# TensorE turns the identity while it waits: 40 transposes ahead of the projection and 42 at the passage to attention

## The chip, the cores and the metric

The kernel runs on one core of a Trainium2 chip. The metric is the device time of one execution in microseconds (us), the median of several runs. In what follows PE is TensorE, PEld its weight loads, ACT ScalarE, DVE VectorE, POOL GpSimd and SP SyncE, which issues most of the DMAs.

## What is computed

A transformer layer over x of 2 x 2048 rows of 256 floats, all in float32: attention with 16 heads of 16, then a mixing projection and a mixture of 8 experts of which each row takes 2, with a layer norm behind each half.

```python
qkv = x @ qkv_w + qkv_b                      # 256 -> 16 heads x (16 q, 16 k, 16 v)
q, k = rot(q), rot(k)                        # the angle depends on the head alone
attn = softmax(q @ k.T / 4)                  # per head, 2048 x 2048
x = layernorm(x + (attn @ v) @ out_w + out_b)
n = layer_norm(x, g1, be1); x2 = x + n + n @ mix_w + mix_b
flat = layer_norm(x2, g2, be2)
combine = top-2 weights of softmax(flat @ router_w)
y = sum over e of combine[:, e] * (silu(flat @ w1[e] + b1[e]) @ w2[e] + b2[e])
out = layernorm(x + x2 + y)
```

## The kernel before

The program has three blocks, one behind the other. At the end of a block every engine drains its work and raises a semaphore; POOL collects these and releases all five engines together. Whoever drains last sets when the next block begins.

**project** (line 176). SP loads rows of x and `qkv_w`; DVE turns the rows (`turn_x`), copies the weights of v and rotates those of q and k in 16 passes (`rotate`: the two 128-row chunks first, then the bias row). PE waits at first for `wv_ready` (the copy of v's weights), multiplies v for the first 512 rows (`take_v(0)`, line 487), then waits for the first `weights_rotated`, takes q of the first rows (`take_qk`, line 497), waits for the second `weights_rotated`, and turns the bias by four transposes (line 538). After that eight groups of 512 rows go through PE, ACT, DVE and POOL, which split q and k in three bf16 parts that SP stores to HBM. POOL makes the identity in its first two microseconds. At the end PE turns `b_in` (line 557) and multiplies a flag (line 559); DVE makes of it `wide`; SP waits until the stores of the parts have landed (lines 239 and 240).

**maxima** (line 600). SP, PE and DVE each load `wide` into a register and branch over the block's body if it is zero, as with this data. ACT and POOL have nothing to do in it.

**attend_route_experts**. PE scores two heads by 512 queries at a time: 8 matmuls of 32 keys each (line 1521) into one of three PSUM buffers; ACT takes the exponential of 128 x 1024 (line 1429) into a ring of six slots; PE weighs v by them (line 1533), 4 matmuls for each exponential, and between these come jobs for the rest of the layer (line 1549). There are 1024 such steps. SP loads the heads of k and q from HBM in the first steps (lines 732, 741, 1063). Behind attention come 71 tiles of the experts (lines 1663, 1676, with transposes at 1542 and 1647), and the last layer norm.

PE's order at the head of attention is written out by hand: four increments of semaphores (lines 1697 to 1700), three scores ahead, and then `attend`, which for each step waits for the exponential, scores three steps ahead and weighs.

Of the kernel before, what the change touches and what calls it, by code (L numbers as in the profile page):

```python
# [15 lines left out]
P = 128  # L16
# [57 lines left out]
def project(nc, dram, keep, hi_all):  # L74

    with ExitStack() as stack:
# [42 lines left out]
        p_qk = [m.ps(f"p_qk{i}", [P, 512]) for i in range(4)]  # L120
# [8 lines left out]
        identity_ready = m.sem("pj_identity_ready")  # L129
# [34 lines left out]
        x_rows = dram["x"].rearrange("b s c -> (b s) c")  # L164
        identity, v_all = keep["identity"], keep["v_all"]
        V_EARLY = QC

        def tokens(g):

# [6 lines left out]
        with nc.Block() as block:  # L176
# [162 lines left out]
            def _(dve):  # L339
# [105 lines left out]
                for g in range(GROUPS):  # L445
# [10 lines left out]
                    if g + 2 < GROUPS:  # L456
                        turn_x(g + 2)
                    if g + 1 < V_EARLY:
                        for i in range(2):
                            add_v(g + 1, i)  # L460
                add_v(V_EARLY, 0)
                read_norms(GROUPS - 1)
# [13 lines left out]
            @block.tensor  # L476
            def _(pe):
                def take_v(g, halves=range(2)):

                    pe.wait_ge(xT_ready, g + 1)  # L480
                    for i in halves:
                        if g:
                            pe.wait_ge(v_ready, 2 * (g - 1) + i + 1)
                        for a in range(2):
                            tok = (2 * i + a) * P
                            for kc in range(KC):
                                last = nc.tensor.matmul(p_v[i][:, a, :], xT[g][:, kc, tok:tok + P],
                                                        w_v[:, kc, :], start=(kc == 0), stop=(kc == KC - 1))
                        last.then_inc(v_done, 1)

                def take_qk(g, ft):

                    if g:
                        pe.wait_ge(rest_ready, 4 * (g - 1) + ft + 1)
                    pe.wait_ge(xT_ready, g + 1)
                    for kc in range(KC):
                        last = nc.tensor.matmul(p_qk[ft][:, :], w_qk[:, kc, ft, :], xT[g][:, kc, :],  # L497
                                                start=(kc == 0), stop=(kc == KC - 1))
                    last.then_inc(qk_done, 1)

                def take_norms(g):

                    if g:
                        pe.wait_ge(norms_read, 2 * g)
                    pe.wait_ge(q_squared, 2 * g + 2)
                    pe.wait_ge(k_squared, 2 * g + 2)
                    for out, first in ((p_x[0], 2), (p_x[1], 0)):
                        for kc in range(KC):
                            last = nc.tensor.matmul(out[:, :], select[:, kc, :, :].rearrange("p r h -> p (r h)"),
                                                    squares[:, g % 2, first + kc, :],  # L510
                                                    start=(kc == 0), stop=(kc == KC - 1))
                    last.then_inc(normed, 1)

                def average(b):

                    pe.wait_ge(mean_ready, b + 1)
                    if b == 0:
                        pe.wait_ge(v_ready, 2 * V_EARLY - 1)
                    else:
                        pe.wait_ge(rest_ready, 4 * GROUPS)  # L520
                    for kc in range(KC):
                        for c in range(QC):
                            last = nc.tensor.matmul(p_mean[b][32 * c:32 * c + 32, :], key_mean[:, b, kc, :],
                                                    hi_all[:, kc, tokens(b * QC + c)],
                                                    start=(kc == 0), stop=(kc == KC - 1))
                    last.then_inc(averaged, 1)

                pe.wait_ge(wv_ready, 1)
                take_v(0)
                pe.wait_ge(weights_rotated, 1)  # L530
                for g in range(GROUPS):
                    take_qk(g, 0)
                    take_qk(g, 1)
                    if g == 0:
                        pe.wait_ge(weights_rotated, 2)
                        pe.wait_ge(identity_ready, 2)
                        for ft in range(4):
                            last = nc.tensor.transpose(p_qk[3][:, ft * P:(ft + 1) * P], w_qk[:, KC, ft, :], identity[:, :])
                        last.then_inc(bias_turned, 1)
                        pe.wait_ge(filled, 7)  # L540
                        pe.wait_ge(bias_ready, 1)
                    if g:
                        take_norms(g - 1)
                    take_qk(g, 2)
                    take_qk(g, 3)
                    if g == QC + 1:
                        average(0)
                    if g + 1 < V_EARLY:
                        take_v(g + 1)
                pe.wait_ge(mean_read, 1)  # L550
                take_v(V_EARLY, (0,))
                take_norms(GROUPS - 1)
                take_v(V_EARLY, (1,))
                average(1)
                take_v(V_EARLY + 1)
                pe.wait_ge(loaded_b1, 16)
                nc.tensor.transpose(p_qk[2][:, 0:P], b_in[:, :], identity[:, :]).then_inc(b1_turned, 1)
                pe.wait_ge(narrow_ready, 1)
                nc.tensor.matmul(p_qk[1][:, 0:1], ones[:, :], narrow[:, :], start=True, stop=True).then_inc(counted, 1)

def quad(q):
# [13 lines left out]
def maxima(nc, dram, keep):  # L576

    with ExitStack() as stack:
# [9 lines left out]
        p_s = [m.ps(f"mx_s{i}", [P, S]) for i in range(2)]  # L589
# [10 lines left out]
        with nc.Block() as block:  # L600

            @block.sync
            def _(sp):
                wide = sp.value_load(keep["wide"][0:1, 0:1], min_val=0, max_val=P)
                with sp.If(wide > 0):
                    sp.wait_ge(keep["stored_mid"][1], 16 * QC)
                    sp.sem_inc(stored, 16)
                    sp.sem_inc(parts_turned, 1)
                    with sp.Fori(0, BH) as bh:
                        sp.wait_ge(parts_turned, bh + 1)  # L610
                        load_head(sp, dram, bh, q_rows, k_rows, loaded)
                        sp.wait_ge(row_ready, bh + 1)
                        sp.dma_start(dram["negmax"][bass.ds(bh, 1), :, :].rearrange("o t (a n) -> (o t a) n", n=P),
                                     turned[:, :]).then_inc(stored, 16)
                    sp.wait_ge(stored, 16 * (BH + 1))
                    sp.dma_start(keep["q_rows"][0][ROWS:ROWS_M, :, :],
                                 dram["negmax"][0:QUAD, :, 0:512].rearrange("h t n -> t h n")).then_inc(stored, 16)
                    sp.wait_ge(stored, 16 * (BH + 2))

            @block.tensor  # L620
            def _(pe):
                wide = pe.value_load(keep["wide"][0:1, 0:1], min_val=0, max_val=P)
                with pe.If(wide > 0):
                    with pe.Fori(0, BH) as bh:
                        pe.wait_ge(loaded, (bh + 1) * (16 * 12))
                        for qt in range(KT):
                            if qt >= 2:
                                pe.wait_ge(reduced, bh * KT + qt - 1)
                            for c in range(QC):
                                last = nc.tensor.matmul(p_s[qt % 2][:, c * 512:(c + 1) * 512],  # L630
                                                        q_rows[0:ROWS, qt * P:(qt + 1) * P],
                                                        k_rows[0:ROWS, c * 512:(c + 1) * 512], start=True, stop=True)
                            last.then_inc(scored, 1)
                        pe.wait_ge(parts_ready, bh + 1)
                        nc.tensor.transpose(p_turn, columns[:, :],
                                            keep["identity16"][:, :]).then_inc(parts_turned, 1)
                        pe.wait_ge(row_ready, bh + 1)
# [110 lines left out]
def attend_route_experts(nc, dram, keep):  # L748
# [24 lines left out]
    with ExitStack() as stack:  # L773
# [11 lines left out]
        p_s = [m.ps(f"at_s{i}", [P, PAIR * 512]) for i in range(BUFFERS)]  # L785
        p_o = m.ps("at_po", [P, 512])
        small = m.ps("at_small", [P, 512])
# [139 lines left out]
        identity = keep["identity"]  # L927
# [65 lines left out]
        with nc.Block() as block:  # L993
# [517 lines left out]
            def _(pe):  # L1511
# [186 lines left out]
                pe.sem_inc(o_copied, 1)  # L1698
                pe.sem_inc(small_read, 1)
                pe.sem_inc(h_ready, 4)  # L1700
                for n in range(BUFFERS):
                    score(0, n)
                attend(0, False, False, 0)
# [421 lines left out]
```

## Time and profile before

| | |
|---|---|
| median of 3 runs | 1629.89 us (1628.8 to 1631.36) |
| the profiled execution's own time | 1633.76 us |
| its span, first to last instruction | 1632.1 us |
| PE busy, share of the span | 96% |
| ACT busy | 75% |
| DVE busy | 36% |
| POOL busy | 28% |
| mean granted clock of TensorE | 0.987 |

### The profile page before, as it was taken

The page shows a single profiled execution, that of the slowest core. Times are in us where ns is not written, and L with a number is a line of the kernel's source. Part 1 is how long each engine was busy: PE and PEld are TensorE (multiplying, and loading weights), DVE is VectorE, ACT ScalarE, POOL GpSimd, SP SyncE. Part 2 cuts the span into 40 slices and gives each one's busy share as a digit, 9 for nine tenths or more (in the row PEclk, how much of TensorE's full clock was granted, in tenths as well). Part 3 has the DMA queues.
Part 4 walks back from the last instruction along what each step waited for, and adds up shares of the span by engine and source line. Part 5 has one row for each costly group of instructions (what it writes and reads, how often), then busy time and mean ns, then how long its engine had stood idle before and what let it go on. Part 6 is the DMA issues. An engine that isn't in the chain of part 4 may idle for free.

```text
span 1632.1 us, 46348 instructions
## 1 busy us (share of the span) xinstructions
PE 1565.6 (96%) x17759; PEld 920.5 (56%) x17763; DVE 594.6 (36%) x1515; ACT 1227.1 (75%) x1818; POOL 463.2 (28%) x431
## 2 busy tenths in 40 slices
PE   7989999999999999999999999999999999999990
PEld 4443433344334334334434434378899999999990
DVE  6641221553553554544544446443630000000004
ACT  4669999999999999999999999953343343433332
POOL 4730010121321221221221221133546444444441
PEclk9999999999999999999999999999999999999995
DMA  6896210220212552321221211869779876667645
GB/s 172 223 166 85 52 41 12 67 57 20 85 57 66 115 111 60 121 57 38 67 57 38 69 55 38 238 173 199 179 169 236 199 201 179 185 191 194 186 111 212
DMA packets 187563, 195.13 MB, mean 120 GB/s; under 512 B 97161, under 2 KB 159433, under 8 KB 187209
## 3 DMA queue, kind: packets, MB, share of 16 engines
q1 hardware_dynamic: 173587, 174.39, 39.3%
q0 software_dynamic: 13296, 17.77, 6.7%
q8 instruction: 128, 2.10, 0.6%
q10 hardware_dynamic: 495, 0.41, 0.1%
q14 instruction: 57, 0.47, 0.1%
HBM read 141.16 MB, written 47.00 MB: 115 GB/s over the span
## 4 chain that ended last, share of the span: by engine, by line
PE 87%; DVE 2%; issue 2%; ACT 2%; DMA 1%; POOL 0%; DVEq 0%; POOLq 0%; ACTq 0%
PE at_s L1521 26%; PE at_po L1533 26%; PE at_s L1663 16%; PE at_s L1676 15%; PE at_small L1549 4%; ACT place L1429 2%; DVE cb_ln_stats L688 1%; DVE late L714 1%; DMA rows_out<-place,at_v 0%; DVE at_o L1752 0%; PE at_po L1647 0%; DMA place<-rows_out 0%; DVE place L1969 0%; PE at_small L1542 0%; ACT place L1446 0%
## 5 line engine op out<-in xcount | busy, mean ns | idle before, releaser
L1429 ACT ACTIVATE place<-at_s 128x1024 f32<-128x1024 f32 x1024 | 950.4, 1119 | 16.8 <-PE at_s L1521 9.5
L1521 PE MATMUL at_s<-place 99*32 99x512 bf16 x8192 | 570.3, 381 | 7.3 <-PEq L600 5.1
L1533 PE MATMUL at_po<-place,at_v 128*32 128x512 f32 x4096 | 534.9, 594 | 6.3 <-DVE at_o L1752 4.3
L1521 PEld LDWEIGHTS at_s<-place 99*32 99x32 bf16 x8192 | 222.6, 96 | 437.0 <-issue 249.0
L1446 ACT ACTIVATE place<-at_s,b_turned 128x128 f32<-128x128 f32 x568 | 162.0, 369 | 146.1 <-PE at_s L1663 139.4
L1663 PEld LDWEIGHTS at_s<-ex_xT,place 128*128 128x128 f32 x2272 | 264.1, 192 | 7.6 <-issue 3.6
L1663 PE MATMUL at_s<-ex_xT,place 128*128 128x128 f32 x2272 | 265.7, 275 | 1.5 <-issue 1.5
L1676 PE MATMUL at_s<-place 128*128 x1136 | 257.3, 380 | 1.4 <-issue 0.7
L1676 PEld LDWEIGHTS at_s<-place 128*128 128x128 f32 x1136 | 210.4, 190 | 28.1 <-issue 2.4
L1533 PEld LDWEIGHTS at_po<-place,at_v 128*32 128x32 f32 x4096 | 131.7, 111 | 105.5 <-POOL at_v L1267 7.6
L1462 ACT ACTIVATE place<-at_s,at_v 128x256 f32<-128x256 f32 x71 | 33.7, 474 | 160.7 <-PE at_s L1676 148.3
L1950 DVE STREAM_TRANSPOSE ex_xT<-at_v 128x256 f32<-128x256 f32 x53 | 23.5, 445 | 333.1 <-PE at_s L1663 313.4
L1267 POOL COPY at_v<-place 128x1024 f32<-128x1024 f32 x32 | 33.4, 1046 | 385.4 <-PE at_po L1533 330.4
L1389 POOL DMA_INDIRECT rows_out<-place,at_v x71 | 113.4, 1597 | 66.1 <-POOL place L1384 53.9
L1384 POOL TENSOR_TENSOR place<-place 128x256 f32<-128x256 f32 x71 | 52.7, 742 | 207.6 <-ACT place L1462 207.3
L1762 DVE RECIPROCAL at_den<-at_den 128x512 f32<-128x512 f32 x32 | 107.3, 3353 | 1.1
L1305 POOL DMA_INDIRECT rows_in<-rt_sent_rows,rt_pos x64 | 64.3, 1005 | 126.0 <-PE at_po L1533 120.5
L1775 DVE TENSOR_TENSOR late<-at_small,rt_total 128x512 f32<-128x512 f32 x32 | 22.1, 692 | 211.5 <-PE at_small L1549 205.2
L1379 POOL TENSOR_TENSOR place<-place,at_v 128x256 f32<-128x256 f32 x71 | 80.2, 1129 | 17.6 <-issue 16.5
L1752 DVE COPY at_o<-at_po 128x512 f32<-128x512 f32 x32 | 22.1, 692 | 145.3 <-PE at_po L1533 142.7
L1289 POOL TENSOR_TENSOR rt_total<-late 128x1024 f32<-128x1024 f32 x7 | 16.7, 2391 | 159.6 <-DVEq L1887 159.6
L295 ACT ACTIVATE place<-p_qk,bias_qk 128x512 bf16<-128x512 f32 x32 | 21.8, 684 | 34.5 <-PE p_qk L497 22.8
(219 smaller groups left out, 949.3 us busy)
## 6 DMA issues: line engine op xcount, KB each, us to landing
place<-in_w SPq DMA_DIRECT2D x61, 1024.0 KB, 11.6
place<-in_w SPq DMA_DIRECT2D x72, 256.0 KB
place<-k_parts SPq DMA_DIRECT2D x48, 256.0 KB, 4.6
place<-q_parts SPq DMA_DIRECT2D x186, 64.0 KB
at_v<-rows_in SPq DMA_DIRECT2D x212, 32.0 KB
late<-kept SPq DMA_DIRECT2D x52, 128.0 KB, 2.6
place<-in_x SPq DMA_DIRECT2D x32, 128.0 KB, 3.2
at_heads_T<-at_o SPq DMA_DIRECT2D x128, 32.0 KB
```

The lines of the kernel that those rows point to most:

```text
L1305: nc.gpsimd.indirect_dma_start(out=dram["rows_in"], in_=sent_rows[:, n, a, :], in_offset=None, out_offset=bass.IndirectOffsetOnAxis(ap=pos ...
L1379: nc.gpsimd.tensor_tensor(biased[:, :], b2[:, bass.ds(e, 1), :].rearrange("p o n -> p (o n)"), rows_now[:, r, D + 1:D + 2].broadcast_to([P ...
L1384: nc.gpsimd.tensor_tensor(y[:, u, :], y[:, u, :], biased[:, :], ALU.add).then_inc(y_ready, 1)
L1389: nc.gpsimd.indirect_dma_start(out=dram["rows_out"], in_=y[:, u, :], in_offset=None, out_offset=bass.IndirectOffsetOnAxis(ap=rows_now[:, r ...
L1429: nc.scalar.activation(probs[:, slot(i, n), :], scores(i, n)[:, :], ACT.Exp).then_inc(exp_done, 1)
L1446: last = nc.scalar.activation(hT[:, u, fc, :], p_h[u][:, fc, :], ACT.Silu, bias=keep["b1"][:, bass.ds(e, 1), fc])
L1521: last = nc.tensor.matmul(scores(i, n)[j:j + 32, s * 512:(s + 1) * 512], k_rows[0:ROWS_M, quad(q).start + h, kt * P + j:kt * P + j + 32], ...
L1533: last = nc.tensor.matmul(p_o[32 * h:32 * h + 32, :], v_one[q % 2][:, h, kt, :], probs[:, slot(i, q * NG + g), s * 512:(s + 1) * 512], sta ...
L1549: last = nc.tensor.matmul(out[j:j + 32, :], weights[:, j:j + 32], moving, start=start, stop=stop, skip_group_check=lone)
L1663: last = nc.tensor.matmul(p_h[u][:, fc, :], w1_now[slot][:, kc, fc * P:(fc + 1) * P], xT[:, u, kc, :], start=(kc == 0), stop=(kc == KC - 1))
L1676: last = nc.tensor.matmul(p_y[u][:, :], hT[:, u, fc, :], w2[:, bass.ds(e, 1), fc, :].rearrange("p o n -> p (o n)"), start=(fc == 0), stop= ...
L1762: v.reciprocal(den[:, :], den[:, :]).then_inc(den_ready, 1)
```

## The change

Four places get transposes of the identity by itself whose results nobody reads: 40 in `project` as soon as POOL has made the identity, ahead of the wait for `wv_ready`; 18 at the end of `project`, behind the last matmul; 8 ahead of the load of `wide` in `maxima` and 8 behind it, ahead of the branch; 8 in the last block between the increments and the first score.

```diff
+        WARMING = 40
...
+                pe.wait_ge(identity_ready, 2)
+                for _ in range(WARMING):
+                    nc.tensor.transpose(p_qk[3][:, 0:P], identity[:, :], identity[:, :])
                 pe.wait_ge(wv_ready, 1)
                 take_v(0)
...
                 nc.tensor.matmul(p_qk[1][:, 0:1], ones[:, :], narrow[:, :], start=True, stop=True).then_inc(counted, 1)
+                for _ in range(18):
+                    nc.tensor.transpose(p_qk[3][:, 0:P], identity[:, :], identity[:, :])
...
             @block.tensor
             def _(pe):
+                for _ in range(8):
+                    nc.tensor.transpose(p_s[1][:, 0:P], keep["identity"][:, :], keep["identity"][:, :])
                 wide = pe.value_load(keep["wide"][0:1, 0:1], min_val=0, max_val=P)
+                for _ in range(8):
+                    nc.tensor.transpose(p_s[1][:, 0:P], keep["identity"][:, :], keep["identity"][:, :])
                 with pe.If(wide > 0):
...
                 pe.sem_inc(h_ready, 4)
+                for _ in range(8):
+                    nc.tensor.transpose(small[:, 0:P], identity[:, :], identity[:, :])
                 for n in range(BUFFERS):
                     score(0, n)
                 attend(0, False, False, 0)
```

## Rows read from the trace of the kernel before

**Rows 1.** The page: busy time by engine, and a group of instructions.

```profile
PE 1565.6 (96%) x17759; PEld 920.5 (56%) x17763; DVE 594.6 (36%) x1515; ACT 1227.1 (75%) x1818; POOL 463.2 (28%) x431
...
L1429 ACT ACTIVATE place<-at_s 128x1024 f32<-128x1024 f32 x1024 | 950.4, 1119 | 16.8 <-PE at_s L1521 9.5
```

**Rows 2.** Windows on PE: length, PE busy (count), clock, DMA share, GB/s.

```profile
10.81:14.74 3.93, 3.93 (x9) 1.00 1.01 268
14.74:16.45 1.71, 1.71 (x9) 1.00 0.22 48
```

**Rows 3.** Timeline, 0 to 21 us: start, length, engine, line, operation, count, idle before.

```profile
1.43 0.53 POOL L249 TENSOR_SCALAR_AFFINE_SELECT identity<-identity 128x128 f32<-128x128 f32 x2 [0.24 <-POOL identity L246]
...
15.22 0.42 DVE L376 TENSOR_TENSOR w_qk<-rot_a,rot_b 128x256 f32<-128x256 f32 x1
...
16.29 3.60 PE L497 MATMUL p_qk<-place,w_qk 128*128 128x512 f32 x8
...
19.77 0.29 DVE L376 TENSOR_TENSOR w_qk<-rot_a,rot_b 128x128 f32<-128x128 f32 x1
...
20.12 0.66 PE L538 MATMUL p_qk<-identity,w_qk 128*128 128x128 f32 x4 [0.24 <-DVE w_qk L376]
```

**Rows 4.** The end of project, line 176: duration in ns, start in us.

```profile
L176 PEldq DRAIN  x1: 1272/1272/1272, 98.5 to 98.5; - x1
...
L176 SPq DRAIN  x1: 7/7/7, 102.0 to 102.0; - x1
```

**Rows 5.** The same for maxima, lines 622 and 600.

```profile
L622 PEldq TENSOR_LOAD <-wide x1: 496/496/496, 102.3 to 102.3; - x1
...
L600 PEldq DRAIN  x1: 64/64/64, 103.6 to 103.6; - x1
L600 DVEq DRAIN  x1: 70/70/70, 103.8 to 103.8; - x1
```

**Rows 6.** Timeline of PE in the experts' stage.

```profile
1089.30 1.28 PE L1663 MATMUL at_s<-ex_xT,place 128*128 128x128 f32 x10
1090.42 0.60 PE L1542 MATMUL at_small<-identity,rt_sent_rows 128*128 128x128 f32 x4
```

**Rows 7.** Line 1671, a register load of PE there, in the same microseconds.

```profile
L1671 PEldq TENSOR_LOAD <-tile_expert x1: 308/308/308, 1089.1 to 1089.1; - x1
```

**Rows 8.** Timeline of PE and ACT at the head of attention.

```profile
104.85 5.31 PE L1521 MATMUL at_s<-place 99*32 99x512 bf16 x48 [5.10 <-PEq L600]
...
105.94 6.73 ACT L1429 ACTIVATE place<-at_s 128x1024 f32<-128x1024 f32 x7 [0.38 <-PE at_s L1521]
112.93 11.22 ACT L1429 ACTIVATE place<-at_s 128x1024 f32<-128x1024 f32 x12 [0.27 <-PE at_s L1521]
124.33 9.27 ACT L1429 ACTIVATE place<-at_s 128x1024 f32<-128x1024 f32 x10 [0.18 <-PE at_s L1521]
136.82 1.94 ACT L1429 ACTIVATE place<-at_s 128x1024 f32<-128x1024 f32 x2 [3.22 <-PE at_s L1521]
139.02 1.94 ACT L1429 ACTIVATE place<-at_s 128x1024 f32<-128x1024 f32 x2 [0.26 <-PE at_s L1521]
141.18 123.79 ACT L1429 ACTIVATE place<-at_s 128x1024 f32<-128x1024 f32 x134 [0.22 <-PE at_s L1521]
...
134.07 1.86 PE L1533 MATMUL at_po<-place,at_v 128*32 128x512 f32 x8 [2.01 <-issue]
```

**Rows 9.** Windows: PE, PEld, DVE, ACT, POOL busy (count), clock, DMA share, GB/s.

```profile
104.85:110.30 5.45, 5.45 (x52) 2.14 (x56) 1.33 (x3) 5.06 (x7) 2.59 (x6) 0.50 0.99 140
110.30:132.06 21.76, 21.75 (x304) 8.90 (x296) 0.00 (x0) 21.21 (x24) 0.00 (x0) 1.00 1.00 127
132.06:134.20 2.14, 0.13 (x4) 0.13 (x8) 0.00 (x0) 1.54 (x2) 0.00 (x0) 1.00 0.53 73
134.20:137.60 3.40, 3.40 (x28) 1.21 (x28) 0.00 (x0) 0.78 (x1) 0.00 (x0) 0.50 0.02 5
```

**Rows 10.** DMA queues from 130 to 132.3 us: packets, MB, share of 16 engines.

```profile
q8 instruction: 1, 0.02, 5.0%
```

## Prediction

> **What bounds the kernel now.** I read the page first, for who is busy: PE is at 96% of the span, and the exponentials of attention alone hold ACT for 950 us [rows 1]. So two engines are close to their limit in attention, and the question for each place of the change is whether PE's speed there moves anything else. For that I read the timeline up to 21 us, the drains at the two block ends, and the timeline of ACT at the head of attention.
>
> Three places show a PE that runs slow or stands still around its idle stretches. The first nine matmuls of the kernel take 3.93 us and the next nine 1.71 us [rows 2], so the first stretch runs at the lower level, 1.2 GHz, though the column still says 1.00. The granted clock was 0.50 from 104.85 to about 110.3, while the first scores ran [rows 9]. And PE stands still for 2.01 us at 132.06 with nothing that a semaphore explains [rows 8], after which the clock is 0.50 again for 3.4 us [rows 9].
>
> What ACT loses by this is read from the starts of its runs of exponentials [rows 8]. From 141.18 on 134 of them take 123.79 us, 0.924 us each, without a gap: there ACT is the bound, and whatever it lost before is lost for good. From 105.94 to 124.33 it does 7 + 12 = 19 in 18.39 us where 19 x 0.924 is 17.56: 0.83 us lost, small gaps in which it waits for scores. From 124.33 to 141.18 it does 14 in 16.85 us where 12.94 would do: 3.91 us lost, by the stand of PE at 132.06 and the slow clock behind it. The start of the first exponential, 105.94, is 1.09 us behind the first score (104.85).
>
> **The change part by part.** *The price of a transpose.* Four of this shape take 0.60 us and one alone about 0.27 [rows 6], so a further one costs (0.60 - 0.27) / 3 = 0.11 us at the full clock, and an estimated 0.22 us at half. Then 8 take 0.11 x 7 + 0.27 = 1.04 us, 18 behind a running matmul add 1.98 us, and 40 add between 4.4 and 8.8 us.
>
> *The first 40.* The identity is there at 1.96 us [rows 3]. They end between 6.4 and 10.8 us (plus the 0.27 of the last), just when the first real matmul begins (10.81), and cost nothing there. What they can bring: `take_v(0)` takes up to 2.1 us less (nine matmuls at 0.44 instead of 0.19 us each). But the q matmuls behind it wait for DVE's rotation, which ends at 15.22 + 0.42 = 15.64 and stood at 16.29 in PE's order; they could start 0.65 us earlier. The four transposes of the bias wait again for DVE, whose second rotation ends at 19.77 + 0.29 = 20.06, and PE was already idle for 0.24 us ahead of them [rows 3]. DVE's passes don't depend on PE. So everything from 20.12 on stays where it is: the gain is 0, bounds 0 and 0. The loss too: if all 40 run at half clock and end at 11.1, `take_v(0)` has 0.65 + 0.24 us of slack before the bias.
>
> *The 18 at the end of project.* PE's drain there ends at 98.5 + 1.27 = 99.8, and SP's begins at 102.0, last of all [rows 4]: it waits for the stores to land. 18 transposes take PE to 99.8 + 1.98 = 101.8. That is still 0.2 us ahead of SP, so they cost 0; bounds 0 and 0.2 (their last one may land later than this).
>
> *The 16 in maxima.* PE's load of `wide` begins at 102.3, and its drain ends at 103.6 + 0.06; DVE's drain is last, 103.8 + 0.07 = 103.9 [rows 5]. A register load is issued while earlier matmuls still stand in the queue: at 1089.1 one ran although ten matmuls of line 1663 began at 1089.30 or later [rows 6, 7]. So the first eight run beside the load and the work behind it, and only the second eight count: issued at about 103.1 to 103.2, they end 1.04 us later, 104.2, and PE drains at 104.3. The block then ends 0.4 us later than by DVE. Bounds: 0.3 if they are issued at once, 1.2 if the load waits for the first eight (102.2 + 1.04 + 0.8 for the load and its checks + 1.04 = 105.1). I take 0.4, since rows 7 is the same instruction in the same queue.
>
> *The 8 ahead of the scores.* They stand on PE's own path: eight times 0.11 is 0.88 us more before the first score. ACT waits for that score; its own table load ends at 105.6, so it has only 0.38 us of cover.
>
> *What the full clock gives back there.* The two groups of matmuls of the first score take half: first score to first exponential falls from 1.09 to about 0.66 us, -0.43. The 0.83 us that ACT lost up to 124.33 goes if PE isn't behind. Both lie between 0 and these values.
>
> Sum of the passage: 0 + 0.4 + 0.88 - 0.43 - 0.83 = +0.02 us. With the bounds it reaches from -0.1 (0.3 for the block end) to +3.1: if the clock falls anyway, the second eight end 2.1 us after 103.2 (1.3 late), the last eight cost 1.76, and nothing comes back.
>
> *The stand at 132.06.* A fetch of instructions lies right ahead of it: one packet of the instruction queue from 130 us on [rows 10], while the data transfers fill the DMA engines (share 1.00 up to 132.06 [rows 9]). PE's 17759 + 17763 instructions over the 128 packets that the page counts on this queue are some 278 for each, an estimate. The change puts 82 transposes, 164 instructions with their weight loads, ahead of the scores. PE issues 304 + 296 instructions in 21.76 us here, 27.6 per us, so the point where the next packet is needed comes some 6 us earlier in attention's order, about 126 us, and the next after it at some 135. Transfers fill the engines up to 132 and at 53% in the two microseconds behind it [rows 9], so the first of these falls in the crowd and the second behind it; rows can't say how early each packet is asked for. So the stand may vanish (-3.91), shrink, or stay (0). I take a third of it, -1.3 us. A second reason for little: the profiled execution took 1633.76 us, 3.87 more than the median, about the size of this loss; the runs without a profile may not have it.
>
> The Trainium skill, "Runtime: NRT & Kernel Launch", section "Instruction fetch mechanics", says that the sequencer fetches the next block of 256 instructions through a DMA queue of its own while it executes the current one, and that a crossing is mostly hidden. The 2.01 us at 132.06 speak against "hidden" where data fills the engines; by the page's rule alone the term would be 0 and the time that of the passage alone, 1629.9 us.
>
> Total: 0.0 + 0.02 - 1.3 = -1.3 us. The profiled execution's 1633.76 would become 1632.5. The median of 1629.89 becomes 1628.6 us.
>
> **The rivals.** *The stand goes altogether.* No packet is late between 105 and 140 us. For it: the share of DMA falls to 0.53 and 0.02 behind 132 [rows 9], so a need 3 us later than before misses the crowd. Against: the crowd is there from 104.85 on, and a packet is needed every 278 / 27.6 = 10 us. Time: -3.9, 1626.0.
>
> *The clock isn't held, or the load waits.* For it: PE still pauses for some half microsecond after each batch, and 8 transposes are short. Against: the 34 transposes up to the end of maxima fill 34 x 0.11 = 3.7 us of what were 5.1 us of idle time before the first score [rows 8]. It costs +1.6 (load waits) to +3.1, 1631.5 to 1633.0.
>
> *One more fetch is late (slower).* The packet needed at about 116 us (10 us ahead of the one at 126) must come through engines that have been full since the first transfer of k [rows 9]; if it arrives a microsecond or more after its need, PE stands as at 132.06 and ACT loses another 3.9 us, with the old stand kept. It decides from there alone, and gives 1633.8 us. Against it: at 122, 10 us ahead of the old stand, a packet was needed in the same crowd and PE didn't stand still (it was busy 21.75 of 21.76 us [rows 9]).
>
> *The change does nothing at all at the start* is the forecast itself.
>
> **How the numbers follow.** The forecast (passage even, stand shrunk by between nothing and most of it) has 0.50; its own range is 1627.0 to 1630.5. The stand gone has 0.24, clock or load 0.14, one more late fetch 0.12. A change under 0.2% (3.3 us) can't be told from none here. Faster: 0.20 of the second case and 0.04 of the first, 0.24. Slower: 0.10 of the last and 0.04 of the third, 0.14. Same: 0.62. The range leaves out the lowest part of the second case and the highest of the last: 1625.8 to 1633.0.
>
> **What would show it.** After: the bias transposes of line 538 at 20.1 us as before; the drain of PE at the end of project at 101.8, ahead of SP's; PE and not DVE the last to drain at the end of maxima, at about 104.3; the first score at 106.1, with the granted clock at 1.00; the first exponential near 106.8; from there 0.92 us for each. A clock of 0.50 at 106 us or a drain of PE at 105 would prove the third case. Idle PE by "issue" over 1 us between 110 and 140 decides the rest, and it is where this forecast is weakest.

## The result, and the profile after

The change made the kernel slower: the median of 20 runs is 1633.15 us, that of the kernel before 1629.95 us in 20 runs beside them, and the ratio is 1.0015 (95% interval 1.0009 to 1.0022), which is 2.4 us; the medians lie 3.2 us apart. Forecast were 1628.6 us and, with a chance of 0.62, a difference that can't be told from none; 1633.15 lies just above the range's end of 1633.0. Two single executions, of 2374 us in e7 and of 8652 us in e8 below, are in no ratio. The profiled execution of the change took 1631.96 us (span 1630.2) and is one of its shorter ones. The profiled execution of before, 1633.76 us, was longer than any of these 20 runs of that kernel (1628.25 to 1633.3). So the two traces stand in the wrong order, and what they show must be read place by place.

The page after, the two lines that answer to [rows 1]:

```profile
PE 1572.3 (96%) x17841; PEld 934.2 (57%) x17845; DVE 596.4 (37%) x1515; ACT 1226.5 (75%) x1818; POOL 461.4 (28%) x431
...
L1439 ACT ACTIVATE place<-at_s 128x1024 f32<-128x1024 f32 x1024 | 949.7, 1121 | 13.7 <-PE at_s L1531 6.4
```

82 more matmuls, and the exponentials wait 3.1 us less for PE in this profile. Now the timeline of PE from the start, against [rows 3]:

```profile
2.02 6.69 PE L531 MATMUL p_qk<-identity 128*128 128x128 f32 x40 [2.02 <-POOL identity L250]
10.25 3.72 PE L488 MATMUL p_v<-late,place 128*128 128x256 f32 x16 [1.54 <-DVE late L383]
15.14 3.70 PE L498 MATMUL p_qk<-place,w_qk 128*128 128x512 f32 x8 [1.17 <-DVE w_qk L377]
19.56 0.65 PE L542 MATMUL p_qk<-identity,w_qk 128*128 128x128 f32 x4 [0.72 <-DVE w_qk L377]
```

The 40 took 6.69 us, 0.17 us each, between the forecast's 0.11 and 0.22. The first 16 matmuls behind them took 3.72 us, not 5.64. The time went into longer idle times ahead of line 498 (1.17 us) and line 542 (0.72 instead of 0.24 us). The first matmul came 0.56 us earlier with its data, and the bias at 19.56 came the same 0.56 us earlier: the speed-up itself gave nothing.

The drains at the end of project (line 177), against [rows 4], and of maxima (line 606), against [rows 5]:

```profile
L177 SPq DRAIN  x1: 7/7/7, 98.6 to 98.6; - x1
L177 PEldq DRAIN  x1: 2163/2163/2163, 99.1 to 99.1; - x1
L177 DVEq DRAIN  x1: 777/777/777, 99.3 to 99.3; - x1
```

```profile
L606 PEldq DRAIN  x1: 788/788/788, 102.7 to 102.7; - x1
L606 DVEq DRAIN  x1: 70/70/70, 103.0 to 103.0; - x1
```

PE is the last at both. At the end of project it is done at 99.1 + 2.16 = 101.2, 1.2 us behind DVE (100.0). SP, which drained at 102.0 before and would have covered that, drains at 98.6. At the end of maxima PE is 0.4 us behind DVE, as forecast. The timeline of PE and ACT behind that, against [rows 8]:

```profile
99.01 0.17 PE L563 MATMUL p_qk<-bd_narrow,bd_ones 128*128 128x1 bf16 x1
99.04 2.16 PE L565 MATMUL p_qk<-identity 128*128 128x128 f32 x18
101.51 1.06 PE L629 MATMUL mx_s<-identity 128*128 128x128 f32 x8 [0.30 <-PEq L177]
102.41 1.08 PE L632 MATMUL mx_s<-identity 128*128 128x128 f32 x8
104.39 1.06 PE L1712 MATMUL at_small<-identity 128*128 128x128 f32 x8 [0.90 <-PEq L606]
105.38 0.83 PE L1531 MATMUL at_s<-place 99*32 99x512 bf16 x12
```

```profile
106.05 56.41 ACT L1439 ACTIVATE place<-at_s 128x1024 f32<-128x1024 f32 x61 [0.80 <-PE at_s L1531]
163.04 97.82 ACT L1439 ACTIVATE place<-at_s 128x1024 f32<-128x1024 f32 x106 [0.59 <-PE at_s L1531]
```

The first exponential follows the first score after 0.67 us (1.09 before), and from there ACT goes through 61 exponentials without a gap in the timeline, until 162.5. The granted clock stayed at 1.00, in windows on PE (length, PE busy and count, clock, DMA share, GB/s), against the first and second row of [rows 9]:

```profile
105.38:110.30 4.92, 4.05 (x61) 1.00 1.07 138
110.30:132.00 21.70, 21.70 (x312) 1.00 0.99 133
```

So in this pair of executions the change is 4.1 us ahead when attention ends: the first matmul of the experts starts at 1068.88, before at 1072.98. Of these 4.1 us it keeps 1.8 to the end. Where the rest goes is in the first tiles of the experts. Before, DVE and then POOL:

```profile
1091.79 2.07 DVE L1764 TENSOR_TENSOR at_o<-at_o,at_den 128x512 f32<-128x512 f32 x1
1090.20 3.11 POOL L1295 TENSOR_TENSOR rt_sent_rows<-late,rt_be 128x512 f32<-128x512 f32 x2
```

After:

```profile
1087.25 4.17 DVE L1776 TENSOR_TENSOR at_o<-at_o,at_den 128x512 f32<-128x512 f32 x1
1087.77 3.10 POOL L1305 TENSOR_TENSOR rt_sent_rows<-late,rt_be 128x512 f32<-128x512 f32 x2
1092.17 0.63 PE L1552 MATMUL at_small<-identity,rt_sent_rows 128*128 128x128 f32 x4 [1.60 <-DVE rt_turned L1781]
```

The same multiply of DVE takes 2.1 us longer. In both profiles it ends 0.56 us behind the end of POOL's two adds (1093.87 and 1093.31; 1091.42 and 1090.87); in the change these adds come 1.7 us later in the work of the experts. PE stands idle for 1.60 us because DVE copies `small` that much later. No transpose of the change is near.

### The profile page after: what moved, and what is told of

Its sections match the earlier page's. It is cut to its first block, busy times and chain, and to the rows that moved or that the text cites. A ratio compares the mean times of both kernels' runs of the same rounds, so it can differ in the third digit from the quotient of the medians.

```text
span 1630.2 us, 46512 instructions
## 1 busy us (share of the span) xinstructions
PE 1572.3 (96%) x17841; PEld 934.2 (57%) x17845; DVE 596.4 (37%) x1515; ACT 1226.5 (75%) x1818; POOL 461.4 (28%) x431
## 4 chain that ended last, share of the span: by engine, by line
PE 85%; DVE 3%; issue 2%; ACT 2%; DMA 1%; SPq 0%; POOL 0%; DVEq 0%; POOLq 0%; ACTq 0%
PE at_po L1543 26%; PE at_s L1531 26%; PE at_s L1673 15%; PE at_s L1686 14%; PE at_small L1559 4%; ACT place L1439 2%; DVE late L724 1%; DVE cb_ln_stats L698 1%; DMA at_v<-rows_in 0%; DMA rows_out<-place,at_v 0%; DVE at_o L1764 0%; DVE at_o L1776 0%; DMA place<-rows_out 0%; DVE at_den L1774 0%; PE at_po L1657 0%
## 5 line engine op out<-in xcount | busy, mean ns | idle before, releaser
L1531 PEld LDWEIGHTS at_s<-place 99*32 99x32 bf16 x8192 | 225.9, 95 | 427.0 <-issue 232.4
```

What stands on the lines that cost most here:

```text
L1531: last = nc.tensor.matmul(scores(i, n)[j:j + 32, s * 512:(s + 1) * 512], k_rows[0:ROWS_M, quad(q).start + h, kt * P + j:kt * P + j + 32], ...
```

## The experiments

A **stand** is in what follows an idle time of PE that the profile puts down to "issue", and a **shift** the number of instructions (two for each transpose) that a kernel adds ahead of a place. **b2** is the load of the experts' biases behind attention, told by the time from its issue to its landing. The expectations speak of three theories. **A, position**: the change puts 164 instructions ahead of attention, so PE needs its next packet of instructions at other moments of the same work, and that alone costs time. **B, work**: the transposes at the passage take time of their own. **C, start**: a fuller PE at the start delays what follows. Each ratio is against the kernel before on the same chip, with a 95% interval. 0.001 is 1.6 us.

**e1_start_only**: the 40 alone.

```diff
+                pe.wait_ge(identity_ready, 2)
+                for _ in range(40):
+                    nc.tensor.transpose(p_qk[3][:, 0:P], identity[:, :], identity[:, :])
                 pe.wait_ge(wv_ready, 1)
```

> Only the 40 transposes at the start, none at the passage. Theory A (position: the added instructions move the points where PE needs its next packet of instructions, and the whole loss is that) : 80 instructions of shift, between before and after, 0 to +2.5 us. Theory B (work: the transposes at the passage cost the 2.4 us): equal to before within 0.5 us. Theory C (the start: fuller PE there delays what follows): +2.4 us, like after.

Measured: 0.9997 (0.9987 to 1.0006). That is against theory C, and a shift of 80 instructions costs nothing that the interval (-2.1 to +1.0 us) would show.

**e2_passage_only**: the 18 + 16 + 8 as in the change, without the 40.

> Only the 18 + 16 + 8 transposes at the passage. Theory A: 84 instructions of shift, 0 to +2.5 us, about as e1. Theory B: +2.4 us, like after. Theory C: as before within 0.5 us.

Measured: 1.0006 (0.9997 to 1.0014), between "none" and the change's 1.0015, and clear of neither: it decides for no theory. Its profile has a stand of PE of its own, at another place of the same work:

```profile
119.17 0.60 PE L1528 MATMUL at_s<-place 99*32 99x512 bf16 x6
121.16 0.82 PE L1528 MATMUL at_s<-place 99*32 99x512 bf16 x10 [1.39 <-issue]
```

**e3_shift_only**: the instructions without the work.

```diff
+                pe.wait_ge(identity_ready, 2)
+                for _ in range(82):
+                    nc.tensor.transpose(p_qk[3][0:32, 0:32], identity[0:32, 0:32], identity[0:32, 0:32])
                 pe.wait_ge(wv_ready, 1)
```

> 82 transposes of 32 x 32 at the start and none elsewhere: the same 164 instructions ahead of attention as the change, with little work and none at the passage; the clock at the first scores should be 0.50 again. Theory A: +2.4 us or more, like after. Theory B and C: as before within 0.5 us. Its profile shows whether PE stands still by issue between 105 and 140 us.

Measured: 1.0014 (1.0005 to 1.0022), the size of the change's loss, with no transpose at the passage: theory A, though the twelve executions spread from 1629.1 to 1634.4 us. The wait at the experts' head is there too:

```profile
1091.12 0.63 PE L1546 MATMUL at_small<-identity,rt_sent_rows 128*128 128x128 f32 x4 [1.47 <-DVE rt_turned L1773]
```

**e4_page_shift**: the change, and 46 transposes of 32 x 32 ahead of the 40.

```diff
+                for _ in range(46):
+                    nc.tensor.transpose(p_qk[3][0:32, 0:32], identity[0:32, 0:32], identity[0:32, 0:32])
```

> The change, and 46 further transposes of 32 x 32 at the start, so that 256 instructions are added ahead of attention in all: by the Trainium skill's page a whole block, which puts the block ends back where they were in attention's order. Theory A: as before within 0.8 us. Theory B and C: +2.4 us, like after.

Measured: 1.0005 (0.9997 to 1.0014), an interval that overlaps that of e3. In its profile, 1634.94 us and the longest of its twelve executions, PE stands where it stood in [rows 8], behind the same matmuls (1.16 us later than there, after a longer stand):

```profile
130.24 1.05 PE L1533 MATMUL at_s<-place 99*32 99x512 bf16 x16
135.23 1.93 PE L1545 MATMUL at_po<-place,at_v 128*32 128x512 f32 x8 [3.94 <-issue]
```

Counted from the first score, a stand begins 26 to 27 us behind it in the profiles with a shift of 0 or 256 instructions (before, e5, e4), 14.1 us behind it at 80 or 84 (e2, and e7 and e10, where the idle time is put down to ACT), and 29 us behind it at 164 (e3, e6, e8, there 0.3 to 0.8 us long). Where it stands goes by the shift. The packet of the instruction queue is served there late as well: it starts 25.6 us behind the first score in the profile before, 25.2 in e5 and 26.7 in e4, and PE resumes 1.3 to 1.8 us after the packet's end; in e11 below, where PE doesn't stand, it starts after 23.1 us. These are the strongest signs that the stand is the fetch of instructions. The Trainium skill, "Runtime: NRT & Kernel Launch", section "Instruction fetch mechanics", gives 256 instructions as the block that the sequencer fetches; the places at 0 and 256 agree with the period. Its "mostly hidden" holds in some executions (no stand in the change, e1, e9 and e11) and not in others: 1.4 to 3.9 us in e2, the profile before, e5 and e4, while the DMA engines are full (share 1.00 in [rows 9]), and 0.3 to 0.8 us in e3, e6 and e8.

**e5_before_again**: the kernel before, unchanged.

> The kernel before, unchanged, timed against itself. A measure of what the comparison can tell: 1.000 within 0.05%. Its profile is a second look at three things of one execution: SP's drain at the end of project (102.0 in the first profile, 98.6 to 101.1 in the four experiments), the stand of PE at 132 us, and the load of b2 behind attention, which by the position theory lands 7.2 us after its issue again, with DVE's multiply at 2.1 us.

Measured: 1.0000 (0.9986 to 1.0013). SP's drain begins at 99.6, not 102.0. b2 lands 7.3 us after its issue and the multiply takes 2.09 us, as expected. PE stands for 2.63 us:

```profile
131.74 1.93 PE L1533 MATMUL at_po<-place,at_v 128*32 128x512 f32 x8 [2.63 <-issue]
```

Its 12 executions fall in two heaps, seven from 1629.38 to 1630.41 and five from 1632.90 to 1634.33 us, with the profiled one (1633.01) in the upper heap. But of 35 others of the same kernel beside them ten lie between the two, so that the heaps are not shown to be more than chance.

**e6_realigned_experts**: the change, with 92 idle increments in groups 4 to 6 of attention.

```diff
                     for n in range(NB):
+                        if i in (4, 5, 6) and n % 4 == 0 and not (i == 6 and n >= 112):
+                            pe.sem_inc(padding, 1)
                         pe.wait_ge(exp_done, i * NB + n + 1)
```

> The change, and 92 increments of a semaphore that nobody waits for, one every fourth step of the groups 4 to 6 of attention, so that 256 instructions are added ahead of the experts and 164 ahead of attention. Position theory: the load of b2 lands after 7.2 us, not 9.6, DVE's multiply takes 2.1 us, not 4.2, PE's wait of 1.6 us for it is gone, and the time falls by 1.5 to 2 us against the change (some 1631.3 for 1633.1). Rival (the wait is chance, or comes from the passage): 4.2 and 1.6 us stay, the time is the change's within 0.5 us or worse by the increments.

Measured: 1.0003 (0.9992 to 1.0014), 1631.78 us. That is 2.0 us under the change's first ratio, as expected, and 0.7 us under its second (e9 below); the intervals overlap, so that the gain in time is not shown. In the profile the expectation held: b2 lands after 7.1 us, the multiply takes 2.09 us again, and PE doesn't wait for DVE:

```profile
1089.52 2.09 DVE L1779 TENSOR_TENSOR at_o<-at_o,at_den 128x512 f32<-128x512 f32 x1
```

**e7_twelve_in_maxima**: 28 at the start and 12 ahead of the load of `wide`; no others.

```diff
             def _(pe):
+                for _ in range(12):
+                    nc.tensor.transpose(p_s[1][:, 0:P], keep["identity"][:, :], keep["identity"][:, :])
                 wide = pe.value_load(keep["wide"][0:1, 0:1], min_val=0, max_val=P)
```

> 28 transposes at the start and 12 in maxima ahead of the load of wide, 80 instructions as in e1_start_only, nothing at the end of project, behind the load or ahead of the scores. If the transposes ahead of the load lie beside it, DVE is last to drain in maxima and the block ends as in e1; if the clock is held, the first exponential comes 0.4 us after e1's distance from the first score (0.66 for 1.09 us) and the time is 0.5 to 1 us under e1's ratio of 0.9997. If the clock falls all the same: as e1. If the load waits for the transposes: 1 us slower than e1.

Measured: 0.9986 (0.9975 to 0.9997), 1628.18 us, faster than the kernel before. PE begins the 12 when the block is released and is through before DVE drains, and the first scores run at the full clock:

```profile
100.60 1.50 PE L627 MATMUL mx_s<-identity 128*128 128x128 f32 x12 [1.14 <-PEq L177]
103.20 1.48 PE L1527 MATMUL at_s<-place 99*32 99x512 bf16 x24 [1.10 <-PEq L604]
```

**e8_no_eighteen**: the change without the 18, and 18 of 32 x 32 at the start in their place.

> The change without the 18 transposes at the end of project, with 18 of 32 x 32 at the start instead, so that all positions stay. If the 18 outlast the stores in most executions, PE drains at 99.2 there instead of 101.2, project ends up to 1.2 us earlier and the time is 0.8 to 1.2 us under the change's. If they are hidden behind SP, as forecast, the time is the change's within 0.3 us.

Measured: 1.0003 (0.9992 to 1.0014), some 2.0 us under the change's ratio of 1.0015 and 0.7 us under that of e9; both differences are within the intervals. The profile shows it more clearly: there project ends by DVE at 100.6, 0.6 us earlier than by PE in the change though its data came 0.5 us later, and SP (100.2) doesn't cover it. 1.0 us of the wait at the experts' head is left.

**e9_change_again**: the change once more.

> The change, unchanged, beside e10 on one chip. Position theory: the load of b2 lands after 9.5 us again and PE waits 1.5 us for DVE behind it; the ratio is 1.0010 to 1.0020. Rival (the wait at the experts' head was chance): 7 us and no such wait.

Measured: 1.0007 (0.9996 to 1.0018), 1632.09 us: half of the first loss, below the range that was expected, and not clear of none by itself. One part of the expectation held: b2 landed after 10.3 us, later than in any other profile. But the multiply took 0.69 us and PE didn't wait. The timeline of DVE and then of POOL:

```profile
1089.30 0.69 DVE L1776 TENSOR_TENSOR at_o<-at_o,at_den 128x512 f32<-128x512 f32 x1
```

```profile
1090.92 3.12 POOL L1305 TENSOR_TENSOR rt_sent_rows<-late,rt_be 128x512 f32<-128x512 f32 x2
```

POOL starts so late here that its adds begin behind the multiply instead of beside it. So a late b2 costs time in some executions of the change and not in others.

**e10_twelve_again**: e7 once more, beside e9.

> e7_twelve_in_maxima once more. If its gain holds, a ratio of 0.9980 to 0.9992, and 3 to 5 us under e9 in the medians; if it was the chip's spread, 0.9995 or more.

Measured: 0.9984 (0.9975 to 0.9993), 1628.05 us, 4.0 us under e9 in the medians. The gain holds.

**e11_before_look**: the kernel before, one execution.

> A third look at the kernel before. The timed runs of it fall in two heaps, some 1629 and some 1633 us. If the heaps are made by the stand of PE near 132 us, a run of about 1629 us shows less than 1 us of it and a run of about 1633 us shows 2 us or more, and all else is alike.

Measured: 1629.1 us, and ACT has no gap of over 0.27 us from 112 to 180 (the timeline of ACT):

```profile
105.57 6.55 ACT L1429 ACTIVATE place<-at_s 128x1024 f32<-128x1024 f32 x7 [0.39 <-PE at_s L1521]
112.40 67.95 ACT L1429 ACTIVATE place<-at_s 128x1024 f32<-128x1024 f32 x73 [0.27 <-PE at_s L1521]
```

Its SP drained late, at 101.6, as in the first profile. The first matmul of the experts starts at 1068.65 here, at 1072.98 in the first profile and at 1072.20 in e5, and from there to the end all three take 558.8 to 559.1 us. So the stand and the slow clock behind it, and not SP, make the difference of 4 us between these executions of the same kernel: 1629.1 us without it, 1633.0 and 1633.8 with it.

What the profiles show side by side, with the instructions added ahead of attention and ahead of the experts. "Passage" is the time from the start of the flag's matmul, the last one that `project` needs, to the first exponential.

| kernel | added | passage, us | largest stand of PE, 105 to 140 us | b2, us | DVE's multiply, us | PE waits for it, us |
|---|---|---|---|---|---|---|
| before, e5, e11 | 0, 0 | 6.36, 4.57, 6.46 | 2.0, 2.6, none | 7.2, 7.3, 7.1 | 2.07, 2.09, 2.05 | none |
| e1 | 80, 80 | 4.99 | none | 5.6 | 2.24 | none |
| e7, e10 | 80, 80 | 4.56, 4.63 | 1.2, 1.3 (put down to ACT) | 6.3, 6.1 | 2.24, 2.20 | none |
| e2 | 84, 84 | 7.04 | 1.4 | 6.1 | 2.24 | none |
| the change, e9 | 164, 164 | 7.04, 7.04 | none | 9.6, 10.3 | 4.17, 0.69 | 1.6, none |
| e3 | 164, 164 | 4.57 | 0.4 | 9.5 | 4.06 | 1.5 |
| e8 | 164, 164 | 5.85 | 0.3 | 9.0 | 3.57 | 1.0 |
| e6 | 164, 256 | 7.20 | 0.8 | 7.1 | 2.09 | none |
| e4 | 256, 256 | 7.04 | 3.9 | 7.2 | 2.08 | none |

From the first matmul of the experts to the end, the nine profiles with a multiply of 2.0 to 2.3 us take 558.7 to 559.1 us, those of the change, e3 and e8 take 561.4, 561.9 and 560.9 us, and that of e9 takes 557.9. So the price of the shift is paid behind attention, 2 to 3 us, of which the wait of PE is 1.0 to 1.6; and e9 doesn't pay it.

## Why the prediction was wrong

**The start was right**: forecast 0, and e1 measured 0.9997. DVE's rotation set the end of that stretch with or without a fast PE.

**"The 18 cost 0" failed.** The step hid them behind SP's drain at 102.0 [rows 4]. That number came from one execution. Counted from the flag's matmul, SP drained 2.4 us later there and 2.5 in e11, but 0.6 us later in e5, the same kernel, and from 0.6 us earlier to 1.9 later in the ten profiles of other kernels. Where SP is early, DVE is last, 1.0 us behind the flag, and PE with its 18 ends 2.2 us behind it. The price of 1.98 us was right; the cover was 0.8 us instead of all of it, so that 1.2 us are paid.

**The rest of the passage was right by its parts**: 0.4 us for the eight behind the load (measured 0.4), 0.88 us for the last eight (0.99), first score to first exponential 0.66 (0.67), clock 1.00. But what the full clock gives back was read off the same execution. In e5, the same kernel without a transpose, that first distance was 0.66 us already, since the clock fell only behind the first score, and nothing is left of the 0.43 us there. And of "0.83 us given back": from the 1st to the 21st exponential the change took 18.30 us, the first profile of before 19.31, but e11 18.98 and e5 18.70. So 0.4 to 1.0 us came back. Altogether the table's passage is 7.0 us with all transposes, and 4.6 us (e5) or 6.4 and 6.5 us in the kernel before; less what comes back, that is a cost of 2.1 us where SP is early and of -0.3 to -0.1 where it is late. Forecast was +0.02. e2 against e1 (0.0009, 1.5 us) and e8 against the change (0.0012, 2.0 us) fit a cost, but each interval is wider than the difference.

**The stand was taken for a loss to be won back, and position for a gain alone.** This is the term of -1.3 us. What was seen rightly: a fetch lies at the stand of [rows 8], and 164 instructions move it. But only some executions have the stand (two of the three profiles of the kernel before), so that it is worth little in a median; the text named this doubt itself (1633.76 is 3.87 over the median) and still took a third. What the text didn't look at is that the same shift moves every later fetch as well, among them one behind attention. Measured in place of -1.3 us: +2.3 us for the shift alone (e3, 1.0005 to 1.0022, or 0.8 to 3.6 us). A shift of a whole block (e4, 1.0005) and the experts put back alone (e6, 1.0003) measured less, within overlapping intervals. The rival "one more fetch is late" had the sign and about the size, and the wrong place: it looked at 116 us, the price is paid at 1090. That a change under 0.2% can't be told from none was wrong too: 20 executions of each kernel told 0.15% from none.

How a shift costs time at 1090 us is shown up to one link. POOL's first operation for the experts waits for b2. Its two adds follow, and in twelve of the thirteen profiles DVE's multiply ends 0.56 us behind the second of them, whether it takes 2.1 or 4.2 us; in e9 the multiply was done before they began, in 0.69 us. The Trainium skill, "SBUF — State Buffer", section "SBUF: two separate sides", says that DVE operations with two inputs in SBUF and GpSimd's that read it share a port pair, and that the one which starts first has it while the other blocks altogether. The 0.69 us of e9 and the 0.56 us behind POOL agree with blocking. The order doesn't in the change and in e3: by its record the multiply begins 0.4 to 0.5 us before POOL's first add, and ends behind the second all the same.

What moves b2 is the link that stays open. The thirteen profiles fall in three groups without an exception, and e6 changed its group by the shift alone. Where a packet of the instruction queue starts 2.2 to 2.7 us behind b2's issue (shift 164), b2 lands after 9.0 to 10.3 us; where it starts 2.1 to 2.4 us ahead of the issue (0 and 256), after 7.1 to 7.3 us; where none starts within 7 us ahead of the issue or while b2 loads (80 and 84), after 5.6 to 6.3 us. Why a packet of 16 KB should hold a load up by 2 us or more is not settled, and no kernel here took the two apart.

Open too: how the 2.4 us (1.1 us in e9) divide between the passage and the experts; why the change's 20 executions beside the result have none below 1631.3, although e9 has 1629.0 and 1630.5; and why e7 measured below e1 (0.9986 and 0.9984 for 0.9997, intervals that overlap) with the same shift. The profiles of e7 and e10 begin their first exponential 0.4 us sooner than e1's and lose that again by their stand of 1.2 us.

## What to carry to other kernels

An engine's slack at a barrier is a difference of two late arrivals, and one trace gives one draw of it. Before work is hidden behind an arrival that waits for DMA, profile a second execution. And instructions added to PE's program are a change of their own: try the same number of instructions with no work in them, and a whole block more, before the work gets praise or blame for a few microseconds. Warming transposes have a chance to pay only where their engine isn't the last to arrive. The kernel with 28 at the start and 12 ahead of the register load, where DVE still drained last, measured 2.3 and 2.6 us under the kernel before; how much of that is the clock and how much the shift of 80 instructions is not shown.

## What the runs showed of the hardware

In the eight profiles with 12 or more transposes of the identity at the passage, the granted clock was 1.00 (2.4 GHz) at the first score and stayed there up to 1594 us; only in e4 was it 0.50 (1.2 GHz) in between, for 3.4 us behind the stand of 3.9 us, as in [rows 9]. In the five without, it was 0.50 for 3.4 or 6.8 us at the head of attention, and in e5 it fell only 0.9 us behind the first score. A register load of PE at 101.5 us ran beside the eight transposes ahead of it. A stand of PE for instructions reached 3.94 us, and came and went between executions of one kernel. And a DVE multiply of 128 x 512 took 0.69, 2.1 or 4.2 us, and ended 0.56 us behind POOL's second add wherever it didn't end before the first began.
